# Second product of a mixer on TensorE: four column halves replaced by zero-padded weights and accumulation over the whole array

## The reference

```python
xh = _dht2d(x).reshape(B, H, W, nb, bs)                   # nb = 8 blocks of bs = 16 channels
xn = jnp.roll(jnp.flip(xh, axis=(1, 2)), shift=(1, 1), axis=(1, 2))
w1a, w1b = (w1[0] + w1[1], w1[0] - w1[1])
o1k = jax.nn.relu(0.5 * (xh @ w1a + xn @ w1b) + b1[0])     # per block
o1n = jax.nn.relu(0.5 * (xn @ w1a + xh @ w1b) + b1[1])
w2a, w2b = (w2[0] + w2[1], w2[0] - w2[1])
o2k = 0.5 * (o1k @ w2a + o1n @ w2b) + b2[0]
o2n = 0.5 * (o1n @ w2a + o2k @ w2b) + b2[1]
y = (o2k + o2n).reshape(B, H, W, C)
y = jnp.sign(y) * jax.nn.relu(jnp.abs(y) - SPARSITY)
return _dht2d(y) / (W * C) + x
```

## Time and profile before

| what | value |
|---|---|
| median of 3 runs | 102.38 us (102.36 to 102.53) |
| profiled execution, device time | 102.17 us |
| its span, first to last instruction | 100.3 us |
| mean granted TensorE clock | 0.997 |
| busy PE / DVE / ACT / POOL | 94.4 / 62.0 / 61.3 / 50.7 us |

### The profile page before, as it was taken

The page is one execution under the profiler, slowest core; times in us unless marked ns, Lnnn a source line. Parts: engine busy times, 40 slices in busy tenths (PEclk is TensorE's granted clock), DMA queues, the critical chain, the costliest instruction groups (busy, mean ns, idle before and its releaser), DMA issues.

```text
span 100.3 us, 2242 instructions
## 1 busy us (share of the span) xinstructions
PE 94.4 (94%) x748; PEld 79.8 (80%) x748; DVE 62.0 (62%) x211; ACT 61.3 (61%) x174; POOL 50.7 (51%) x99
## 2 busy tenths in 40 slices
PE   5979999999999999999999999999999999999950
PEld 4547778999989888987779778989898989897720
DVE  1022843895869858765778659783769765757230
ACT  3213696678677439776559849966178746866400
POOL 1012999804506342250404484988788958943400
PEclk9999999999999999999999999999999999999998
DMA  1999700000000000000000000000000010111121
GB/s 45 260 317 389 300 0 7 0 0 0 0 10 3 0 0 7 0 0 0 0 7 3 0 0 0 7 0 0 0 0 3 0 58 1 52 52 52 58 99 52
DMA packets 3178, 4.46 MB, mean 45 GB/s; under 512 B 608, under 2 KB 2272, under 8 KB 3168
## 3 DMA queue, kind: packets, MB, share of 16 engines
q1 hardware_dynamic: 2016, 3.34, 9.6%
q10 hardware_dynamic: 1152, 0.99, 3.4%
HBM read 3.28 MB, written 1.05 MB: 43 GB/s over the span
## 4 chain that ended last, share of the span: by engine, by line
PE 90%; DMA 5%; issue 1%; DVE 1%; POOL 0%; ACTq 0%; POOLq 0%
PE banks L677 15%; PE banks L612 12%; PE banks L646 11%; PE banks L671 8%; PE banks L626 7%; PE banks L725 5%; DMA values<-in_values 5%; PE banks L575 4%; PE banks L751 4%; PE banks L738 4%; PE banks L558 4%; PE banks L693 4%; PE banks L589 3%; PE banks L707 2%; PE banks L709 2%; PE banks L767 2%
## 5 line engine op out<-in xcount | busy, mean ns | idle before, releaser
L436 POOL TENSOR_TENSOR probs<-probs,inverse 128x256 f32<-128x256 f32 x32 | 19.0, 614 | 11.6 <-DVE inverse L1265 11.5
L424 POOL TENSOR_SCALAR acts<-first,layer 64x260 f32<-64x260 f32 x8 | 9.8, 1220 | 19.6 <-DVE first L1317 19.6
L1014 ACT ACTIVATE probs_t<-banks 128x512 f32<-128x512 f32 x24 | 14.3, 595 | 8.0 <-PE banks L646 7.9
L677 PE MATMUL banks<-probs_t,v 128*128 128x256 f32 x64 | 16.9, 386 | 0.8 <-DVE stream L1289 0.6
L646 PE MATMUL banks<-ident,probs 128*128 128x128 f32 x96 | 14.8, 276 | 0.0
L1007 ACT ACTIVATE probs<-banks,lowest 128x256 f32<-128x256 f32 x32 | 14.0, 489 | 0.0
L646 PEld LDWEIGHTS banks<-ident,probs 128*128 128x128 f32 x96 | 11.2, 141 | 2.6 <-issue 1.1
L677 PEld LDWEIGHTS banks<-probs_t,v 128*128 128x128 f32 x64 | 10.9, 190 | 2.6 <-issue 1.6
L1248 DVE TENSOR_REDUCE lowest<-banks 128x2 f32<-128x512 f32 x16 | 10.5, 682 | 2.7 <-PE banks L575 2.7
L1020 ACT ACTIVATE v<-banks 128x256 f32<-128x256 f32 x16 | 6.2, 393 | 7.5 <-PE banks L612 7.5
L1007 ACT ACTIVATE probs<-negated,lowest 128x256 f32<-128x256 f32 x16 | 7.9, 498 | 2.3 <-DVE negated L1256 2.3
(11 more groups left out here) (110 smaller groups left out, 199.5 us busy)
## 6 DMA issues: line engine op xcount, KB each, us to landing
out<-stream SPq DMA_DIRECT2D x7, 128.0 KB, 1.9
rows<-in_x_rows SPq DMA_DIRECT2D x1, 768.0 KB, 9.0
xt_in<-in_x_t SPq DMA_DIRECT2D x2, 256.0 KB, 4.1
xt_in<-in_x_t SPq DMA_DIRECT2D x1, 512.0 KB, 5.6
constants<-in_constants SPq DMA_DIRECT2D x1, 462.0 KB, 7.4
layer<-in_layer ACTq DMA_DIRECT2D x1, 320.5 KB, 9.0
rows<-in_x_rows ACTq DMA_DIRECT2D x1, 256.0 KB, 7.1
layer<-in_layer ACTq DMA_DIRECT2D x1, 102.0 KB, 9.0
```

Of the source, the lines that this page charges most:

```text
L424: pool.tensor_scalar(acts[H2:C, image, 1], partners(flat(first[H2:C, image]), SUMS, -SUMS, SUMS), column["b1n"][H2:C], 0.0, ALU.add, ALU.m ...
L436: pool.tensor_tensor(probs[:, at, tile, :], probs[:, at, tile, :], inverse[:, at, tile:tile + 1].to_broadcast([TILE, TOKENS]), ALU.mult).t ...
L677: mm = nc.tensor.matmul(mixed_bank, for_job[:, m, 0:C], turned[:, m, :], start=(m == 0), stop=(m == TILES - 1))
L1014: nc.scalar.activation(flat(probs_t[:, i]), probs_t_bank(job), ACT.Copy).then_inc(probs_t_ready[n], 1)
```

## The change

The weight of each half is widened from 64 to 128 columns, with zeros in the columns of the other half. Each product then covers all 128 output channels, and the two halves of a tile are accumulated in PSUM: `start` on the first, `stop` on the second. The number of matmuls stays as it is. GpSimd clears the widened weight once at the start, DVE waits for that and copies the two 64-column pieces separately.

```diff
-        stacked = sb("stacked", [C, 2, H2])
+        stacked = sb("stacked", [C, 2, C])
...
             def norm_scales(pair):
...
-                pool.wait_ge(pool_constants, 1)
+                pool.wait_ge(pool_constants, 2)
...
             pool.memset(minus_half[:, :], -0.5).then_inc(pool_constants, 1)
+            pool.memset(stacked[:, :, :], 0.0).then_inc(pool_constants, 1)
             gate_values0()
...
                 for tile, (start, step) in enumerate(((0, SUMS + skip), (HALF[0], SUMS))):
+                    o = y_bank[:, tile * TILE:(tile + 1) * TILE]
                     for half in range(2):
-                        o = y_bank[half * H2:(half + 1) * H2, tile * TILE:(tile + 1) * TILE]
                         mm = nc.tensor.matmul(
                             o.rearrange("p (a b) -> p a b", a=2), stacked[:, half],
                             partners(flat(acts[:, i, half]), start, step, TILE // 2),
-                            start=True, stop=True)
+                            start=(half == 0), stop=(half == 1))
...
                 elif name == "stacked":
-                    nc.vector.tensor_copy(flat(stacked[:, :, :]), b[:, 0:C]).then_inc(
-                        mixer_ready, 1)
+                    dve.wait_ge(pool_constants, 2)
+                    for half in range(2):
+                        own = slice(half * H2, (half + 1) * H2)
+                        copied = nc.vector.tensor_copy(stacked[:, half, own], b[:, own])
+                    copied.then_inc(mixer_ready, 1)
```

## The result

The changed kernel takes 103.9 us (median of 4 runs, 103.5 to 104.17) against 102.38 before (4 runs); the ratio of the means is 1.0142, with a 95% interval of 1.0106 to 1.0178, so it is slower by 1.1 to 1.8 us. The forecast was 103.7. The profiled execution took 103.5 us with a span of 101.7. The edits move the lines of PE and ACT by one and DVE's last ones by four: the second product is L726, `mix_values` L672, the last step of DVE L1293.

What follows compares the result with a forecast made beforehand. PE was taken to bound the stretch with the second products. Its passes add 1.28 us and a wait at image 3 0.06, all else 0: 102.38 + 1.34 = 103.7 us, range 103.1 to 104.3.

Steps and rivals of the forecast that it cites:

- The bound: From 28 to 52 us, around the eight second products, PE is full, so its time is the kernel's time.
- The old price: Column-half second product: 0.59 us in its piece plus 0.19 in the group behind, 0.78 an image.
- The new price: Eight whole-array passes: 0.89 us, +0.11 for six images; images 6 and 7, behind part-array steps, 1.09, +0.31 each.
- Sum on PE: All eight second products together: PE needs 0.66 + 0.62 = +1.28 us.
- the mixer's stretch was to grow: Sign in the changed trace: the mixer's stretch longer by 1.2 to 1.4 us, stretches behind it unchanged in length.
- the one on waits: At image 3 the old change of form hides a wait for ACT's activation: 0.06 us, bounds 0 and 0.11.
- the price of the later results: Products end 0.20 us nearer their readers, tightest backward_channels of image 7: price 0, up to 1.6 if cover were gone.
- The edits off the path: POOL's memset (0.40 to 0.8 us), DVE's wait and two copies (0.28 to 0.56) are covered: cost 0.
- closer passes: Rival: passes within the second product closer than 0.111 us, faster below 0.091, 100.4 or 101.7 us; chance 0.05.
- nothing changes: Rival: leaving the strips costs nothing behind them and a pass takes 0.098 us, so all balances; chance 0.04.
- taken up behind the mixer: Rival: PE's 0.6 us wait on DVE at the tail absorbs part, giving 103.1 us; chance 0.08.
- The rival of the later waits: Later results bring waits into the mixer's stretch, likely three or four of 0.1 to 0.2, 104.1 to 104.6 us; chance 0.13.

Runs made afterwards that it cites:

- e2: Changed kernel with only the first half of each second product, four whole-array passes in place of eight: 101.34 us, ratio 0.9894 against the kernel before.
- e3: Kernel before with only the first of the two column halves, four passes in place of eight: 102.28 us, ratio 0.9986.
- e4: Kernel before with a second PSUM bank for y of images 1, 3, 5 and second products of 1-2, 3-4, 5-6 back to back: 102.49 us, ratio 0.9989.
- e6: Changed kernel with images 6 and 7 back to column halves: 103.12 us, ratio 1.0057 against the kernel before; changed kernel beside it 103.87.
- e5: Changed kernel with image 3's second product moved behind backward_tokens of image 0: 104.04 us, ratio 1.0141 against the kernel before; changed kernel beside it 103.87.
- e1: Changed kernel with matmuls back to column halves, keeping widened weight, memset, wait and two copies: 102.53 us, ratio 0.9999 against the kernel before.
- e7: Kernel before with second products paired, one more y bank, and PE and ACT steps moved into the waits this opened: 102.24 us, ratio 0.9965.

## Why the prediction was right

The time lies in the range and 0.2 from the forecast, and the terms on PE came out as stated. The bound: PE is full in the stretch, and its own passes set the length to within the waits below; where PE's work was cut by 3.6 us (e2), ACT and DVE took over, so the statement holds for a PE that gets more to do, not for one that gets much less.

The old price of 0.78 us an image: e3 shows both parts of it, 0.44 for four slots whatever number of passes stands in each, and e4 shows the 0.34 as a price for going in and out, paid once for a pair. The new price: 0.89 for six images (0.89 in the chain, image 3 apart), 1.09 for the two behind the projections, as the row from layer 0 said; e6 gives 0.64 back for the 0.62 of that term. Sum on PE 1.28, measured with all that came with it 1.49, a little more than the 1.2 to 1.4 us by which the mixer's stretch was to grow; behind it nothing changed, as stated.

The step that was too small is the one on waits. For image 3 I took 0.06 of at most 0.11; the piece is 1.02 against 0.89, 0.13, above that bound. The timeline after, with ACT's activation ending at 38.90 + 0.51 = 39.41 and the first pass 0.10 behind it:

```profile
38.90 0.51 ACT L1038 ACTIVATE acts<-first,layer 64x260 f32<-64x260 f32 x1
...
39.51 0.35 PE L726 MATMUL banks<-acts,stacked 128*128 128x128 f32 x1
```

Before, the distance was 0.14. That e5 brings the piece to 0.89 supports the wait. The first pass starts 0.10 us ahead of its piece in the chain, where that of image 0 starts 0.16 ahead (28.18 against 28.34): 0.06 late, as much as I took. The other 0.07 lies in that pass, whose row is 0.35 us long against 0.28 for image 0; I had counted only the late start. Both are time of the kernel: without the wait, e5 is 0.12 us shorter.

And I set the price of the later results to 0, with image 7 as the tightest reader. There it held, just: DVE's `shrink` ends at 53.93 and PE starts at 54.09, 0.16 later, in a chain that shows no wait:

```profile
53.45 0.48 DVE L1312 SCALAR_TENSOR_TENSOR normed<-banks,y_bias,xt_in 128x256 f32<-128x256 f32 x1 [0.90 <-ACT xt_in L1047]
...
54.09 0.28 PE L739 MATMUL banks<-constants,normed 128*128 128x128 f32 x1
```

The reader that I missed is `mix_values` of image 6, 0.99 for 0.89. It waits for DVE's residual of the image before:

```profile
30.62 0.80 DVE L1284 SCALAR_TENSOR_TENSOR rows<-banks,inverse,rows 128x128 f32<-128x128 f32 x2
...
31.57 0.35 PE L672 MATMUL banks<-v,probs_t 128*128 128x129 f32 x1
```

DVE's residual ends at 31.42, and PE starts 0.15 later, the usual distance, again with a first pass of 0.35. Image 0's later result reaches DVE over two steps of ACT, `shrink_top` and, next in ACT's order, the copy of the sums (L1030) that DVE's step ahead of the residual waits for. Both waits are there in the timelines, first the kernel before, then the changed one:

```profile
29.05 0.47 ACT L1046 ACTIVATE xt_in<-banks,y_bias 128x256 f32<-128x256 f32 x1 [0.17 <-PE banks L725]
...
29.72 0.29 DVE L1315 TENSOR_TENSOR first<-of_sums,banks 128x130 f32<-128x130 f32 x1 [0.86 <-ACT of_sums L1029]
```

```profile
29.27 0.47 ACT L1047 ACTIVATE xt_in<-banks,y_bias 128x256 f32<-128x256 f32 x1 [0.47 <-PE banks L726]
...
29.95 0.29 DVE L1319 TENSOR_TENSOR first<-of_sums,banks 128x130 f32<-128x130 f32 x1 [1.16 <-ACT of_sums L1030]
```

Each engine waits 0.30 us longer, which is the 0.89 - 0.59 of the product. On top of that the residual takes 0.80 us where it took 0.61; why is open. The piece is 0.97 to 0.99 in the four traces with eight whole-array passes for image 0 (the changed kernel twice, e5, e6) and 0.89 to 0.90 in the five with column halves; no experiment changes image 0 alone. So waits cost 0.13 + 0.10 = 0.23 in place of 0.06: 1.28 + 0.23 = 1.51, against 1.49. (Two further pieces differ by 0.04 us, one up and one down.)

The edits off the path cost nothing that shows, as stated (e1). POOL's memset took 0.31 us, between my bounds, and was done 21 us ahead of the copy that waits for it; the two copies took 0.34, 0.06 more than the one copy:

```profile
0.74 0.31 POOL L480 MEMSET stacked<- 128x256 f32 x1
...
22.08 0.34 DVE L1213 COPY stacked<-banks 128x64 f32<-128x64 f32 x2
```

Of the rivals, closer passes is out by the timeline, 0.11 us apart; "nothing changes" by the result, and "taken up behind the mixer" by the equal 40.85 us behind it. The rival of the later waits is true in part: the prediction named a wait beyond 0.1 us ahead of image 3 as its sign, and 0.13 is there, with a second place that the prediction didn't have. In size it stayed at 0.23 us in place of the 0.4 and more that the rival took as likely, which is why the time lies at the upper end of the forecast's own 103.5 to 103.9.

## What to carry to other kernels

Where a matmul uses half of the array's columns, count it in pairs and count the way in and out: here, for float32 passes of 128 moving columns, 0.11 us a pair plus 0.34 for the change, against 0.11 a pass on the whole array. So eight passes favour the halves (0.78 to 0.89), four would not by an estimate from these numbers (0.22 + 0.34 to 0.45), and products that already stand next to part-array work favour them strongly (0.31 us each). Before changing the form, see whether such products can stand together, and look at the same time for the engine that then falls behind; most of the 1.0 us that three pairs save here went into waits for DVE and ACT. When a result comes later, follow it through every engine that reads it, not only to its nearest reader: here it came back to PE through ACT and DVE. On an engine that is full, compare the work done in a stretch or the length from one landmark to the end, not the busy share.

## What the runs showed that I had not expected

The start of the first product differs by 0.6 us between traces that should agree up to there: 28.34 and 28.25 for the changed kernel, 28.52, 28.75 and 28.88 for e3, e6 and e1. In six traces (the kernel before, the changed one twice, e5, e6 and e7) the chain begins with the load of `values0`, which is of different length; the changed kernel, the same again, and e6:

```profile
1.16 4.53 DMA values<-in_values
```

```profile
1.15 4.45 DMA values<-in_values
```

```profile
1.16 4.94 DMA values<-in_values
```

The 0.49 us between the last two is nearly the whole difference of their first products' starts, 28.25 and 28.75, and in all six the first product starts 22.65 to 22.67 us behind the load's end. The chains of e1 and e3 begin with PE's warm-up instead, and their later starts aren't explained here. The difference would have hidden the gain of e6 had I compared its span with that of the kernel beside it (101.5 and 101.6) instead of lengths behind the first product.
